# Six staging buffers for the weight sums, and the first ternarization pass on ScalarE

## What is computed

```python
# attention: 16 heads of 64, blocks of 128 queries, each sees its own and both neighbour blocks (|distance| <= 128)
scores = einsum(qb, kb) / 8;  scores = where(band, scores, -inf)
out = softmax(scores) @ vb ;  out @ wo + bo
# feed-forward, 1024 -> 4096 -> 1024
act_quant(x)    = clip(round(x * s), -128, 127) / s,   s = 127 / max|x| per token
weight_quant(w) = clip(round(w * s), -1, 1) / s,       s = 1 / mean|w| over the whole matrix
h = act_quant(x) @ weight_quant(w1).T
h = silu(depthwise_conv1d(h, 3 taps) + conv_b)
y = act_quant(h) @ weight_quant(w2).T
```

## Time and profile before

| | |
|---|---|
| median of 3 runs | 2007.9 us (2000.7 to 2016.9) |
| profiled execution, its own time | 2002.15 us |
| its span, slowest core (0) / quickest core (4) | 2000.6 / 1980.8 us |
| TensorE busy, mean granted clock | 1229.7 us (61%), 0.759 |
| VectorE busy | 981.8 us (49%) |
| ScalarE busy | 557.3 us (28%) |
| GpSimdE busy | 65.9 us (3%) |
| moved by DMA | 281.8 MB, mean 141 GB/s |
| reductions of the weight sums | 64 x 1.22 us on VectorE |
| pass 1 / 2 / 3 of the ternarization | 64 x 0.749 / 0.684 / 0.683 us on VectorE |

### The profile page before, as it was taken

How to read it: one execution, slowest core, us unless ns; L and a number is a source line. 1 busy time by engine, 2 the same in 40 slices (tenths; PEclk the granted TensorE clock), 3 DMA queues, 4 the chain that set the end, 5 groups by cost and what they waited for, 6 DMA issues and landing times.

```text
span 2000.6 us, 23274 instructions; the slowest of 8 cores (1980.8 to 2000.6 us)
## 1 busy us (share of the span) xinstructions
PE 1229.7 (61%) x6850; PEld 625.8 (31%) x6850; DVE 981.8 (49%) x2332; ACT 557.3 (28%) x1256; POOL 65.9 (3%) x128
## 2 busy tenths in 40 slices
PE   2299933555569944434177786676767687464545
PEld 1144411111123312212055562433435352331122
DVE  3563684666664437777100366362543625363442
ACT  1233102222335521111035460523324150412100
POOL 2000000000000000000000000000000000000000
PEclk9999975555555557777589898788888898566588
DMA  8398045555550032333656444544454454433044
GB/s 143 116 282 223 1 149 167 161 176 189 191 188 1 1 79 55 77 82 68 155 179 242 158 148 148 184 174 156 160 175 162 147 198 150 158 111 131 24 176 147
DMA packets 97857, 281.83 MB, mean 141 GB/s; under 512 B 28611, under 2 KB 45380, under 8 KB 80198
## 3 DMA queue, kind: packets, MB, share of 16 engines
q1 hardware_dynamic: 79878, 188.88, 29.2%
q0 software_dynamic: 17856, 91.46, 15.2%
HBM read 258.51 MB, written 33.56 MB: 146 GB/s over the span
## 4 chain that ended last, share of the span: by engine, by line
PE 23%; DMA 14%; issue 6%; DVE 5%; ACT 4%; DVEq 0%; ACTq 0%; SPq 0%; POOL 0%; POOLq 0%
PE pA L932 8%; PE pM L1001 8%; DMA w1h<-w1b 7%; DMA w2b<-w2b 7%; PE pC L961 5%; ACT H L967 2%; DVE out L1015 1%; ACT Ab L943 1%; DVE x4b L1036 1%; DVE stat L1019 1%; DVE stat L1021 0%; PE pX L1119 0%; ACT L1025 0%; DVE out L1030 0%; PE pX L1084 0%
## 5 line engine op out<-in xcount | busy, mean ns | idle before, releaser
L932 PE MATMUL pA<-x3w,w1h 128*128 128x256 bf16 (+1 forms) x2304 | 293.1, 275 | 93.2 <-DMA w1h<-w1b 90.8
L1067 DVE TENSOR_REDUCE apar<-H 128x256 f32<-128x2048 f32 x32 | 116.4, 3640 | 434.1 <-ACT H L967 434.1
L1001 PE MATMUL pM<-w2b,H2q 128*128 128x512 bf16 x1024 | 245.9, 399 | 65.9 <-DMA w2b<-w2b 65.9
L932 PEld LDWEIGHTS pA<-x3w,w1h 128*128 128x128 bf16 x2304 | 221.8, 104 | 140.8 <-issue 99.2
L961 PE MATMUL pC<-Ab,diag 128*128 128x256 bf16 x768 | 151.6, 314 | 132.8 <-ACT H L967 89.1
L627 ACT ACTIVATE expm<-psc,negC 128x384 bf16<-128x384 f32 (+1 forms) x256 | 144.7, 567 | 243.2 <-PE psc L620 239.6
L588 PE MATMUL pod<-VA,expm 128*128 128x65 bf16 x768 | 102.1, 237 | 119.4 <-DVE B L598 77.2
L943 ACT ACTIVATE Ab<-pA,mwc 128x256 bf16<-128x256 f32 (+1 forms) x288 | 129.3, 449 | 151.3 <-PE pA L932 146.0
L1001 PEld LDWEIGHTS pM<-w2b,H2q 128*128 128x128 bf16 x1024 | 101.0, 102 | 212.0 <-issue 113.1
L715 PE MATMUL po<-wo,B1all 128*128 128x512 bf16 x256 | 82.8, 495 | 137.0 <-ACT B1all L701 111.0
L967 ACT ACTIVATE H<-pC,cbs 128x256 f32<-128x256 f32 x256 | 120.3, 470 | 73.5 <-PE pC L961 72.3
(11 more groups left out here) (135 smaller groups left out, 1204.5 us busy)
## 6 DMA issues: line engine op xcount, KB each, us to landing
w1h<-w1b POOLq DMA_DIRECT2D x72, 1024.0 KB, 5.2
w2b<-w2b SPq DMA_DIRECT2D x64, 1024.0 KB, 5.3
wstage<-w1t SPq DMA_DIRECT2D x64, 512.0 KB, 6.4
wstage<-w2t SPq DMA_DIRECT2D x64, 512.0 KB, 5.9
xin<-x SPq DMA_DIRECT2D x16, 512.0 KB, 3.8
w1b<-tern2b SPq DMA_DIRECT2D x64, 128.0 KB, 2.2
w2b<-tern2b SPq DMA_DIRECT2D x32, 256.0 KB, 2.2
xre<-x SPq DMA_DIRECT2D x16, 512.0 KB, 5.4
```

Source lines behind the costliest of these rows:

```text
L932: last = p.op("tensor", lambda e, j=j, hs2=hs2, d=d, slotp=slotp, mv=mv, width=width: e.matmul(pA[slotp][:, 0:width], w1h[j % 2][:, d * 51 ...
L1001: last = p.op("tensor", lambda e, sm=sm, hcx=hcx, tsl=tsl, ofs=ofs, b=b, qq=qq, slot=slot: e.matmul(pM[slot][:, :], H2q[sm % 2][:, hcx * 2 ...
L1067: apar_d[s][g3] = p.op("vector", lambda e, g3=g3: e.reduce_max(apar[:, g3 * 256:(g3 + 1) * 256], H2.ap().rearrange("p (c n) -> p n c", c=H ...
```

## The change

Two edits. The weight sums in `b2_qkv` get six staging buffers instead of four, with two more semaphores; a load waits for the reduction of the piece six before. In `tern_steps`, pass 1 becomes an activation on ScalarE (Identity, scale from `swc`, and 128 as its bias from a new constant `rcc`), which counts up ScalarE's semaphore; pass 2 on VectorE waits for that. Passes 2 and 3, loads, stores and the order of the lists stay as they are.

```diff
-    sW = [Sem(nc, f"sW{i}") for i in range(4)]
+    sW = [Sem(nc, f"sW{i}") for i in range(6)]
...
+    rcc = alloc("rcc", [128, 1], F32)
...
+    p.op("vector", lambda e: e.memset(rcc[:], RC), inc=sV)
...
-    wstage = [alloc(f"wstage_{i}", [128, 1024], F32) for i in range(4)]
+    wstage = [alloc(f"wstage_{i}", [128, 1024], F32) for i in range(6)]
...
     def emit_piece(idx):
         src, width = piece_srcs[idx]
-        slot = idx % 4
-        wl = [(sV, red_done[idx - 4])] if idx >= 4 else []
+        slot = idx % 6
+        wl = [(sV, red_done[idx - 6])] if idx >= 6 else []
...
                     wl = [(sW[slot], lds[k])]
                     if tstate.get("u16", [0, 0])[k % 2]:
                         wl.append((sV, tstate["u16"][k % 2]))
-                    n1s[k] = p.op("vector", lambda e, slot=slot, wi=wi, k=k: e.tensor_scalar(
-                        out=tern_u16[k % 2][:, :], in0=wstage3[slot][:, :],
-                        scalar1=swc[:, wi:wi + 1], scalar2=RC, op0=ALU.mult, op1=ALU.add),
-                        waits=wl)
+                    n1s[k] = p.op("scalar", lambda e, slot=slot, wi=wi, k=k: e.activation(
+                        out=tern_u16[k % 2][:, :], in_=wstage3[slot][:, :],
+                        func=AF.Identity, bias=rcc[:], scale=swc[:, wi:wi + 1]),
+                        waits=wl, inc=sS)
                     yield
                 for k in pair:
                     slot = k % 4
                     n2s[k] = p.op("vector", lambda e, slot=slot, k=k: e.tensor_scalar(
                         out=wstage3[slot][:, :], in0=tern_u16[k % 2][:, :],
                         scalar1=RD, scalar2=1.0, op0=ALU.subtract, op1=ALU.min),
-                        waits=[(sV, n1s[k])])
+                        waits=[(sS, n1s[k])])
```

More of the change, by code:

```diff
@@ L477, in build_nc @@
     free(*[f"wsb{s}_{c}" for s in range(2) for c in range(NC)],
-         "wstage_0", "wstage_1", "wstage_2", "wstage_3",
+         "wstage_0", "wstage_1", "wstage_2", "wstage_3", "wstage_4", "wstage_5",
          "pq_0", "pq_1", "pq_2", "pq_3", "pms")
```

## The result

| | before | after |
|---|---|---|
| median of all runs (10 each) | 2013.5 us | 1991.0 us |
| ratio after / before, 95% interval | | 0.9868 (0.9836 to 0.990) |
| profiled execution, span of the slowest core | 2000.6 us | 1976.1 us |
| span, mean of the cores | 1993.8 us | 1971.5 us |

The change makes the kernel 1.3% faster; by the ratio that is 26 us of the 2007.9 given at first, so 1981 where 1984 was forecast; the interval runs from 20 to 33 us. (The ratio leaves out executions in which a die ran slower as a whole; the medians hold them, which is why both are above the first times.)

What follows compares the result with a forecast made beforehand. Loads bound the weight-sum tail, and a loop of VectorE passes and load wait bounds attention with ternarization. Gains of 4.8 + 19.2 = 24 us take the 2007.9 us median to 1984, range 1966 to 2002.

Steps and rivals of the forecast that it cites:

- The loop: Attention with ternarization: per four tiles, 11.2 us of VectorE work, then 6.7 us until a load lands, sets the time.
- Size of the pass: Pass 1 as a ScalarE activation, 128x1024 f32 to int16: 1.25 us each, between 1.01 and 1.37.
- that rival: ScalarE in attention: Identity and Exp need different tables, loads add 61 us, time 2045; chance 0.03.
- the int16 output: Pass 1 on ScalarE: rival that int16 output slows it, at 2.5 us each time 2043; chance 0.04.
- The walk: One ternarization group followed instruction by instruction: ends at 375.5 instead of 376.75, 1.25 us gained, 1.2 taken per group.
- The tail: End of the weight sums after V: six buffers leave 18 loads at 297 GB/s, gain 4.8 us, bounds 3.7 and 11.7.
- the rival in which the rate rises until the reductions are the limit: Tail of the weight sums: gain 11.7 us instead of 4.8, time 1977; chance 0.05.
- The 358 GB/s: Tail of the weight sums: by this rule 18 loads take 26.4 us, reductions limit, gain 11.7; judged not to agree.

Runs made afterwards that it cites:

- e5: Changed kernel with the next group's loads issued right behind the stores of this group's pair with the same buffers; ratio to before 0.9597, ternarization 191.3 us.
- e3: Changed kernel with pass 1 on ScalarE only for the first pair of each group's four tiles; ratio to before 0.9887, ternarization 261.1 us.
- e4: Changed kernel with pass 1 on ScalarE only for the second pair of each group's four tiles; ratio to before 0.9814, ternarization 248.5 us.
- e8: Changed kernel with loads issued half a group ahead and ternarization spread over all 288 attention steps; ratio to before 0.9486.

## Why the prediction was right

**The loop was the right picture.** The forecast read the wait for the loads, the passes of VectorE and SyncE's order as one chain, and took no gain where VectorE was merely less busy. 64 passes of 0.749 us, 46.6 us, left VectorE; 18.6 us came out. e5 shows the chain directly, e3 and e4 show which of its links counts.

**Size of the pass.** 1.25 us were built from three rows; it takes 1.234. Identity ran without a new table load, so that rival fell, and the int16 output costs ScalarE nothing that could be seen. (Both stand in the groups above: L526 at 1234 ns, and one table load, for the exp of L629, as before.)

**Size per group.** The walk gave 9.98 us from the first pass 1 to the last pass 3 (before 11.23 in that group); the mean of 16 groups and 8 cores is 9.88, and 11.15 before: 1.27 gained, where 1.25 was walked and 1.2 taken. Of this 0.11 came back in the time until the next load. Its parts: the first pair brings 0.41, the second 0.86. The walk had VectorE wait for ScalarE before pass 2 of tile 3, by about 0.5 us. It does so in 80 of the 128 groups, by 0.31 us, which is 0.19 in the mean. Another 0.16 goes to a wait that the walk did not have, for the stores that still read `tern2b`. So that the walk met the mean to 0.02 us is in part luck: one wait was put too long and another left out. VectorE of core 0 in order of time, in one group of the changed kernel:

```profile
357.29 0.68 DVE L533 TENSOR_SCALAR wstage<-tern_u 128x1024 f32<-128x1024 int16 x1
358.28 0.69 DVE L533 TENSOR_SCALAR wstage<-tern_u 128x1024 f32<-128x1024 int16 x1 [0.31 <-ACT tern_u L526]
...
359.61 1.29 DVE L544 TENSOR_SCALAR tern2b<-wstage 128x1024 bf16<-128x1024 f32 x2 [0.17 <-issue]
```

The second line is tile 3's pass 2, which starts when ScalarE is done. From one group's first pass 1 to the next are 15.82 us, where it was 16.98 before (forecast 16.0 and 17.2). 16 x 1.2 = 19.2 was forecast, 18.6 measured.

**The tail was sized too small.** 4.8 us forecast, from the rows of core 0; 6.0 measured in the mean of the cores and 7.2 on core 0 (41.0 to 33.8). The term that was off is the rate: I took 297 GB/s, the best slice before, because the DMA share there was 1.00. But with six loads in flight a core gets more at the same share. Core 2 from 280 to 300 us, before and then after:

```profile
280.00:300.00 20.00, 0.00 (x0) 0.00 (x0) 14.05 (x12) 0.00 (x0) 0.00 (x0) 0.50 1.00 300
```

```profile
280.00:300.00 20.00, 0.00 (x0) 0.00 (x0) 15.05 (x14) 0.00 (x0) 0.00 (x0) 0.50 1.00 323
```

In this stretch the mean of the eight cores was 291 GB/s before (261 to 302, mean share 0.95) and is 319 after (313 to 327, mean share 1.00). From the landing of the first load issued in the tail to that of the last are 34.4 us before (20 loads) and 28.2 after (18 loads), 290 and 316 GB/s in the mean of the cores. At the forecast's 297 these last 18 landings would have taken 30.0, and that difference, 1.8 us in the mean and 2.3 on core 0 (27.7), is what the rate was wrong by. So this part went some way toward the rival in which the rate rises until the reductions are the limit; it didn't get there, since the reductions still waited 5.0 us for loads on core 0. The 358 GB/s of the Trainium skill's "HBM Reference" (section "Specifications") were not reached in this tail; 327 is the most that a core of the changed kernel has over these 20 us.

**What I did not see.** That the wait at the end of the loop was worth three times what the moved pass brought (247.2 to 191.3 us), and that spreading the ternarization over all of attention, with nothing else done to the changed kernel, was worth about as much (365 to 303 us from the first pass 1 to the end of attention). The prediction had its price (6.7 us in a group) and its cause (loads behind stores in one queue), and used it only as a thing that stays.

## What to carry to other kernels

Before moving work off a busy engine, find the loop that the work lies on and ask for each instance whether it stands in the loop's wait or behind it: here half of the moved passes stood in a wait and were worth a quarter of the others. If the loop ends in a wait for a transfer, first look at what the transfer stands behind in its queue, and whether it could be issued half a round earlier; with the loads issued earlier, the move was worth little. And an in-order engine that is given an instruction waiting for a DMA passes that wait on to everything behind it.

## What the runs showed of the hardware

The DMA share is no measure of how much more the DMA engines can move. With loads of 512 KB and all cores at it, core 2 had 300 GB/s at a share of 1.00 with four loads in flight and 323 at 1.00 with six; the mean of the cores was 291 and 319. A rate over a fixed stretch of time misleads where the cores don't start together: over 275 to 300 us core 1 of the changed kernel has 292 GB/s, because its first load of the tail lands only at 280.1:

```profile
275.00:280.00 5.00, 0.00 (x0) 0.00 (x0) 5.00 (x5) 0.00 (x0) 0.00 (x0) 0.50 0.83 187
280.00:300.00 20.00, 0.00 (x0) 0.00 (x0) 14.99 (x14) 0.00 (x0) 0.00 (x0) 0.50 0.99 319
```

ScalarE writes int16 from f32 at the rate of its other outputs: 1.234 us for 128x1024 with pointers for scale and bias, against 1.25 worked out from bf16 and f32 rows. TensorE's granted clock stayed at 0.50 (1.2 GHz) over the 230 us of e8 in which it was 95% busy, as it had in the kernel before at 98%; why these stretches are not granted the higher level was not tried.
